# Half of z through another PSUM bank, copied raw, and one product with C fewer on GpSimd in every second group

## What is computed

```python
xz = x @ W_in                                  # x: the layer-normed tokens
xi, z = jnp.split(xz, 2, axis=-1)              # 512 channels each
xc = silu(causal_conv(xi, 4 taps) + conv_b)
dt, Bm, Cm = jnp.split(xc @ W_x, [16, 32], axis=-1)
delta = softplus(dt @ W_dt + b_dt)
h = exp(delta * A) * h + delta * Bm * xc       # for each of 16 states, over the tokens
y = sum_n(h * Cm) + xc * D
out = (y * silu(z)) @ W_out
```

## Time and profile before

| what | us |
|---|---|
| median of 3 runs | 1730.51 |
| lowest, highest | 1729.14, 1731.21 |
| the profiled execution | 1728.77 |
| its span, first to last instruction | 1726.7 |
| busy: PE | 1480.7 (86%) |
| busy: DVE | 1555.7 (90%) |
| busy: ACT | 1331.9 (77%) |
| busy: POOL | 1564.6 (91%) |
| mean granted TensorE clock | 0.947 |

### The profile page before, as it was taken

One profiled execution on the slowest core, in us unless ns is written; L12 is line 12 of the kernel. 1 busy time (PEld: TensorE's weight loads), 2 busy tenths in 40 slices (PEclk: granted clock), 3 DMA queues, 4 the chain that ended last, 5 costly groups with the idle time before them and its releaser, 6 DMA issues.

```text
span 1726.7 us, 28038 instructions
## 1 busy us (share of the span) xinstructions
PE 1480.7 (86%) x9868; PEld 1065.4 (62%) x9868; DVE 1555.7 (90%) x1389; ACT 1331.9 (77%) x3100; POOL 1564.6 (91%) x782
## 2 busy tenths in 40 slices
PE   7778898889888988898889889888889898977688
PEld 7555666666666666666666666666666666654355
DVE  2599999999999999999999999999999999999944
ACT  2577788888888888888888888888888888886644
POOL 0699999999999999999999999999999999999814
PEclk9888999999999999999999999999999999997899
DMA  4667755555656655656666555566665555656110
GB/s 141 138 135 180 163 130 123 122 131 132 145 129 146 132 123 122 131 130 146 129 146 135 122 125 126 130 146 129 145 138 121 125 126 129 142 119 141 36 34 15
DMA packets 194430, 218.47 MB, mean 127 GB/s; under 512 B 94011, under 2 KB 184773, under 8 KB 193778
## 3 DMA queue, kind: packets, MB, share of 16 engines
q1 hardware_dynamic: 193522, 215.51, 56.6%
q0 software_dynamic: 576, 1.17, 0.3%
q10 hardware_dynamic: 192, 0.01, 0.0%
HBM read 169.92 MB, written 47.09 MB: 126 GB/s over the span
## 4 chain that ended last, share of the span: by engine, by line
DVE 41%; ACT 18%; issue 16%; PE 13%; POOL 10%; DMA 2%; SPq 0%; DVEq 0%; ACTq 0%; POOLq 0%
DVE psum L1307 20%; DVE xr L1307 16%; ACT psum L1010 6%; POOL xr L1646 6%; POOL xr L1654 3%; PE psum L610 3%; DVE xr L1316 3%; ACT L1132 2%; PE psum L697 2%; PE psum L782 2%; ACT L1041 2%; ACT soft L1062 2%; ACT soft L1066 2%; ACT soft L1058 2%; PE psum L783 1%
## 5 line engine op out<-in xcount | busy, mean ns | idle before, releaser
L1646 POOL TENSOR_TENSOR xr<-u,bbc 128x912 f32<-128x912 f32 x512 | 1075.5, 2133 | 14.3 <-DMA u<-u_scratch 13.9
L1010 ACT ACTIVATE psum<-delta,a_neg 128x228 f32<-128x228 f32 x2048 | 805.9, 441 | 221.6 <-DVE xr L1316 191.2
L1307 DVE TENSOR_TENSOR_SCAN psum<-psum,xr 128x912 f32<-128x912 f32 x320 | 656.2, 2051 | 68.5 <-ACT psum L1010 59.8
L1654 POOL TENSOR_TENSOR xr<-xr,cbc 128x912 f32<-128x912 f32 x192 | 409.2, 2131 | 31.9 <-DVE xr L1307 28.5
L1307 DVE TENSOR_TENSOR_SCAN xr<-psum,xr 128x912 f32<-128x912 f32 x192 | 392.3, 2043 | 0.0
L1316 DVE TENSOR_TENSOR xr<-psum,cbc 128x912 f32<-128x912 f32 x320 | 353.7, 1105 | 11.1
L711 PE MATMUL psum<-xr,fold 128*32 128x228 f32 x4096 | 295.1, 385 | 50.6 <-POOL xr L1654 26.7
L610 PE MATMUL psum<-xh,win 128*128 128x228 f32 x1024 | 222.7, 367 | 61.8 <-ACT xs L1041 33.4
L610 PEld LDWEIGHTS psum<-xh,win 128*128 128x128 f32 x1024 | 192.1, 193 | 91.7 <-ACT xs L1041 44.0
L661 PE MATMUL psum<-xi,conv_d 128*128 128x228 f32 x1024 | 210.9, 358 | 0.0
L711 PEld LDWEIGHTS psum<-xr,fold 128*32 128x32 f32 x4096 | 96.9, 112 | 178.1 <-issue 79.4
(11 more groups left out here) (204 smaller groups left out, 1574.7 us busy)
## 6 DMA issues: line engine op xcount, KB each, us to landing
delta<-delta_scratch SPq DMA_DIRECT2D x256, 228.0 KB, 6.5
u<-u_scratch SPq DMA_DIRECT2D x256, 228.0 KB, 4.2
bbc<-bc_scratch SPq DMA_DIRECT2D x128, 114.0 KB, 2.6
u_scratch<-u SPq DMA_DIRECT2D x64, 228.0 KB, 4.9
cbc<-bc_scratch SPq DMA_DIRECT2D x128, 114.0 KB, 2.7
delta_scratch<-delta SPq DMA_DIRECT2D x64, 226.0 KB, 5.7
out<-ob SPq DMA_DIRECT2D x32, 228.0 KB
h_scratch<-h SPq DMA_DIRECT2D x31, 228.0 KB
```

What stands on the lines that cost most here:

```text
L1010: ins = nc.scalar.activation(slot(k)[:, j * TOK:(j + 1) * TOK], delta4[:, c // 2, j, c % 2], ACT.Exp, scale=a_neg[:, c, j, n:n + 1])
L1307: nc.vector.tensor_tensor_scan(x if k in ON_POOL else slot(k), slot(k), x, 0.0, ALU.mult, ALU.add).then_inc(scan_done, 1)
L1646: nc.gpsimd.tensor_tensor(xr[:, k % XRING], u4[:, c // 2, :, c % 2], bbc[:, p, n].unsqueeze(1).to_broadcast([P, J, TOK]), ALU.mult).then_i ...
L1654: nc.gpsimd.tensor_tensor(xr[:, k % XRING], xr[:, k % XRING], cbc[:, p, k % NI].unsqueeze(1).to_broadcast([P, J, TOK]), ALU.mult).then_inc ...
```

## The change

Two things are changed. **Half 1 of z** of group g goes into bank BB in place of CB, and is projected right behind unit 7 of the group before, once the transposed rows of the FFN (`x2t`) are copied out of BB. ScalarE copies it as it is into `sz` (`z_copy`, new) behind exponentials 12, and in the window silus it in place, from `sz` to `sz`. `proj_x` half 1, which uses BB next, moves from behind unit 7 to behind unit 8 and waits for that copy. `h2_copy` moves one unit earlier, to 11. There are two counters for z in place of one; waits on `sz_done` are counted anew, and CB is free for tokens after `x_silu` half 0.

**The products with C on GpSimd** are units 1, 3, 8, 10, 12, 13 in even groups (13 in place of 14) and 3, 8, 10, 12, 14 in odd ones (1 is left to VectorE).

```diff
-ON_POOL = (1, 3, 8, 10, 12, 14)
+ON_POOL = (1, 3, 8, 10, 12, 13)
+ON_POOL_ODD = (3, 8, 10, 12, 14)
...
             def z_bank(half):
-                return pair((AB, CB)[half])
+                return pair((AB, BB)[half])
...
                     def bank_c(g):
 
-                        need(pe, xs_done, 2 * g)
-                        need(pe, sz_done, 2 * (g - 1))
+                        need(pe, xs_done, 2 * g - 1)
...
                     def proj_x(g, p, half):
                         if half == 0:
                             pe.wait_ge(xh_done, g + 1)
-                        elif runs(g - 4):
-
-                            pe.wait_ge(x2t_ev, g - 3)
-                        else:
-                            need(pe, delta_done, 2 * g)
+                        elif g >= 1:
+
+                            pe.wait_ge(zc_ev, g)
...
                     def proj_z(g, p, half):
 
-                        if half == 1 and runs(g + 1):
-                            pe.wait_ge(xs_done, 2 * g + 3)
+                        if half == 1 and runs(g - 3):
+                            pe.wait_ge(x2t_ev, g - 2)
                         elif half == 1:
-                            pe.wait_ge(sz_done, 2 * g)
-
+                            pe.wait_ge(delta_done, 2 * g + 2)
...
-                            if k == 13 and runs(i + 1):
-                                proj_z(i + 1, 1 - p, 1)
...
-                            if k == 7 and runs(i + 2):
+                            if k == 7 and runs(i + 1):
+                                proj_z(i + 1, 1 - p, 1)
+                            if k == 8 and runs(i + 2):
                                 proj_x(i + 2, p, 1)
...
-                    def z_silu(g, p, half):
-                        act.wait_ge(z_mm, 2 * g + 1 + half)
-                        need(act, y_done, CH // 2 * (g - 2) + half + 1)
-                        nc.scalar.activation(sz[:, p, 2 * half:2 * half + 2], z_bank(half), ACT.Silu).then_inc(sz_done, 1)
+                    def z_copy(g, p):
+                        act.wait_ge(z_mm[1], g + 1)
+                        need(act, y_done, CH // 2 * (g - 1))
+                        nc.scalar.activation(sz[:, p, 2:], z_bank(1), ACT.Copy).then_inc(zc_ev, 1)
+
+                    def z_silu(g, p):
+                        act.wait_ge(z_mm[0], g + 1)
+                        need(act, y_done, CH // 2 * (g - 2) + 1)
+                        nc.scalar.activation(sz[:, p, 0:2], z_bank(0), ACT.Silu).then_inc(sz_done, 1)
+                        act.wait_ge(zc_ev, g + 1)
+                        nc.scalar.activation(sz[:, p, 2:], sz[:, p, 2:], ACT.Silu).then_inc(sz_b_done, 1)
...
-                            if k == 12 and runs(i - 1):
+                            if k == 11 and runs(i - 1):
                                 h2_copy(i - 1)
...
+                            if k == 12 and runs(i + 1):
+                                z_copy(i + 1, 1 - p)
```

More of the change, by code:

```diff
@@ L49, in fusion_kernel, with on_pool, on_dve, pool_before @@
     E = gate_w.shape[2] - 1
-    ON_DVE = tuple(k for k in range(UNITS) if k not in ON_POOL)
-    N_DVE, N_POOL = len(ON_DVE), len(ON_POOL)
+    def on_pool(i):
+        return (ON_POOL, ON_POOL_ODD)[i % 2]
+    def on_dve(i):
+        return tuple(k for k in range(UNITS) if k not in on_pool(i))
+    def pool_before(i):
+        return sum(len(on_pool(g)) for g in range(i))
+    def dve_before(i):
+        return UNITS * i - pool_before(i)
     bc_scratch = nc.dram_tensor("bc_scratch", (2, 2 * NS, TOK), F32, kind="Internal").ap()
@@ L237, in ffn_free @@
                 elif g == GROUPS - 1:
-                    e.wait_ge(z_mm, 2 * GROUPS)
+                    for half in range(2):
+                        e.wait_ge(z_mm[half], GROUPS)
             def ffn_bank(g):
@@ L344, in fusion_kernel @@
             xs_done = sem("xs_done")
-            z_mm = sem("z_mm")
+            z_mm = [sem("z_mm%d" % half) for half in range(2)]
+            zc_ev = sem("zc_ev")
             sz_done = sem("sz_done")
+            sz_b_done = sem("sz_b_done")
             dbl_mm = sem("dbl_mm")
@@ L436, in product_done @@
             def product_done(e, i, k):
-                if k in ON_POOL:
-                    e.wait_ge(c_pool, N_POOL * i + ON_POOL.index(k) + 1)
+                if k in on_pool(i):
+                    e.wait_ge(c_pool, pool_before(i) + on_pool(i).index(k) + 1)
                 else:
-                    e.wait_ge(c_dve, N_DVE * i + ON_DVE.index(k) + 1)
+                    e.wait_ge(c_dve, dve_before(i) + on_dve(i).index(k) + 1)
             with nc.Block() as block:
@@ L677, in proj_z @@
                             pe.wait_ge(delta_done, 2 * g + 1)
-                        project(p, z_bank(half), (CH + 2 * half) * P).then_inc(z_mm, 1)
+                        project(p, z_bank(half), (CH + 2 * half) * P).then_inc(z_mm[half], 1)
                     def proj_bcdt(g, p):
@@ L693, in proj_delta @@
                         else:
-                            need(pe, sz_done, 2 * g - 1)
+                            need(pe, sz_done, g)
                         for half in range(2):
@@ L739, in h2_turn @@
                         else:
+                            pe.wait_ge(zc_ev, GROUPS)
                             pe.wait_ge(x2t_ev, g)
@@ L752, in ffn_in @@
                             pe.wait_ge(scan_done, UNITS * GROUPS)
-                            pe.wait_ge(c_dve, N_DVE * GROUPS)
+                            pe.wait_ge(c_dve, dve_before(GROUPS))
                         for a in range(2):
@@ L763, in v_center @@
                         if runs(g + 3):
-                            pe.wait_ge(sz_done, 2 * g + 7)
+                            pe.wait_ge(sz_done, g + 4)
                         elif g == GROUPS - 3:
@@ L789, in bias_rows @@
                         pe.wait_ge(pool_c, 4)
-                        pe.wait_ge(sz_done, 2 * GROUPS)
+                        pe.wait_ge(xs_done, 2 * GROUPS)
                         for x in range(E):
@@ L801, in before_first @@
                         var(1)
+                        proj_z(0, 0, 1)
                         for half in range(2):
@@ L805, in before_first @@
                             convolve(1, half)
-                        for half in range(2):
-                            proj_z(0, 0, half)
+                        proj_z(0, 0, 0)
                     def after_last():
@@ L1004, in exps @@
                         step = i if k >= SLOTS else i - 1
-                        if back in ON_POOL:
+                        if step < 0 or back in on_pool(step):
                             need(act, scan_done, v - SLOTS + 1)
                         else:
-                            need(act, c_dve, N_DVE * step + ON_DVE.index(back) + 1)
+                            need(act, c_dve, dve_before(step) + on_dve(step).index(back) + 1)
                         for j in range(J):
@@ L1015, in center_out @@
                         act.wait_ge(cent_mm, g + 1)
-                        need(act, z_mm, 2 * g - 2)
+                        for half in range(2):
+                            need(act, z_mm[half], g - 1)
                         nc.scalar.activation(xh[:, p], pair(CB), ACT.Copy).then_inc(cent_done, 1)
@@ L1129, in window @@
                         if runs(i):
-                            z_silu(i, p, 0)
-                            z_silu(i, p, 1)
+                            z_silu(i, p)
                         act.preload_act_table_set("natural_log_exp_and_others")
@@ L1144, in before_first @@
                         rstd_out(1)
+                        z_copy(0, 0)
                         x_out(1, 0)
@@ L1306, in scan @@
                         x = xr[:, k % XRING].rearrange("p j t -> p (j t)")
-                        nc.vector.tensor_tensor_scan(x if k in ON_POOL else slot(k), slot(k), x, 0.0,
+                        nc.vector.tensor_tensor_scan(x if k in on_pool(i) else slot(k), slot(k), x, 0.0,
                                                      ALU.mult, ALU.add).then_inc(scan_done, 1)
                     def times_c(i, p, k):
-                        if k in ON_POOL:
+                        if k in on_pool(i):
                             return
-                        if k == ON_DVE[0]:
+                        if k == on_dve(i)[0]:
                             dve.wait_ge(c_in, 16 * NQ * (i + 1))
@@ L1650, in times_c @@
                     def times_c(i, p, k):
-                        if k == ON_POOL[0]:
+                        if k == on_pool(i)[0]:
                             pool.wait_ge(c_in, 16 * NQ * (i + 1))
@@ L1684, in body @@
                         for k in range(UNITS):
-                            if runs(i) and k in ON_POOL:
+                            if runs(i) and k in on_pool(i):
                                 times_c(i, p, k)
```

## The result

The change is **slower**: 1776.64 us median (1767.15 to 1783.22, 4 runs) against 1729.83 us before (1729.1 to 1731.21, 4 runs), a ratio of 1.0265 with a 95% interval of 1.0217 to 1.0313. The sign is the one forecast, the size is not: +47 us where +21 was said, and the time lies above the range. The profiled execution took 1777.87 us, with a span of 1776.1 us.

The account below looks back on a forecast made before the run. Bound: VectorE's queue plus its 1.78 us wait for ScalarE before scan 2. Clock +1.2, window -0.42: +0.78 us in 29 groups, -1.5 us for two others, together +21 us: 1751 us, range 1713 to 1764.

Parts of the forecast that it names:

- The sign: Whole kernel: slower, 1751 us against a median of 1730.51; slower by over 0.2% had a chance of 0.62.
- The window and the products: ScalarE's silu window loses its 0.77 us wait for z; the extra VectorE product fits the idle time, cost 0.
- Of the 0.77 us only 0.42 are kept: Scan 4 on VectorE: the centred v does not move with y, so 0.42 us a group are gained.
- TensorE's wait: Before skip_w, with nothing left that does not need y: 2.8 us or more at a stretch, was 0.88.
- The fall of the clock behind it: TensorE's clock falls to 0.50 about when y comes out, over skip_w, fold and centring; path slowed in most groups: 0.57.
- if a low stretch of 3.4 us covers only its start or its end: TensorE's 1.8 us path from y to centred v: about 0.9 us longer then, 1.75 at half speed throughout.
- come up to 1.7 us later ... so I add nothing there: TensorE's tokens, B and C, centring of x: exponentials 6 have 1.6 us in hand, so no cost.
- the path to the centred v at 1.2 us: TensorE's skip_w, fold and centring behind y: 1.2 us longer a group, bounds 0 and 1.75.
- The count: The 29 groups with a centred v (3 to 31) each lose 0.78 us, +22.6 us together.
- Rival 1: The clock holds where y is awaited: 13.7 us gained, 1717 us; chance 0.21.
- Groups 1 and 2: The two early groups without a centred v keep the whole 0.77 us each, -1.5 us together.
- Rival 4: Middle of the group slips, exponentials 13 or 14 late: 0.5 us a group; 1745 us, 1765 with the clock; chance 0.06.

Follow-up runs that it names:

- runs 1 and 6: The kernel before with only the new product sets: 1726.94 us; the change with five unread matmuls in TensorE's wait for y and the old six products: 1709.91 us.
- run 5: The change with five unread matmuls in TensorE's wait for y, and ScalarE's square of the centred v moved behind exponentials 3: 1698.39 us.
- run 3: The change with five unread 228-column matmuls put into TensorE's wait for y, nothing left out: 1709.63 us.
- run 8: The change with the five unread matmuls behind the centring of v, ahead of the tokens, so after the wait for y: 1783.33 us.
- run 9: The change with two unread 228-column matmuls in TensorE's wait for y: 1756.0 us.

## Why the prediction was right and wrong

**The window and the products: right.** Measured from the start of the second y product, the exponentials of state 2 end 0.84 us earlier, and the wait of 1.78 us is 0.93 us. The in-place silu takes 0.61 us, not 0.55. In the window ScalarE no longer waits for half 1 of z; it waits for that projection at the raw copy instead (18.6 us in 26 waits). VectorE does not feel it there: in the short group it idles only ahead of scans 2 and 4. The products cost nothing (runs 1 and 6).

**"Of the 0.77 us only 0.42 are kept": right.** Measured 0.48 us a group where the clock holds (49.26 to 48.78), and 0.38 us more when the square is moved (run 5).

**TensorE's wait: right in one kind of group only.** I reckoned 2.8 us or more. It is 2.60 to 3.36 us ahead of 13 of the 15 long groups and 1.97 to 2.35 us ahead of the 13 short ones. **The fall of the clock behind it: right in kind**, and shown by run 3.

**The size: wrong, in two steps.** The first is "if a low stretch of 3.4 us covers only its start or its end": I took one stretch of 3.4 us, the length that the earlier trace rows shows, for what it would be here too. Behind y it lasts 10.2 us in eleven groups and 13.7 in four. In the earlier trace rows broad matmuls followed (projections, `out_proj`); here the tokens and B and C follow, which use 72 columns of data or 48 of the 128 outputs at a time. Run 8 shows that five broad matmuls ahead of them bring the clock back sooner; which property of the light ones keeps it down, no run separates.

The second step, and the larger, is "come up to 1.7 us later ... so I add nothing there". In the long groups with a centred v the copy of B and C starts 4.4 to 5.7 us later against y. It stands in ScalarE's queue ahead of exponentials 5, and it had nothing in hand, as the trace of before shows: B and C end at 714.40, and their copy starts at 714.44.

```profile
712.66 1.74 PE L685 MATMUL psum<-xs,wx 128*48 128x228 f32 x8
```

```profile
714.44 0.35 ACT L1052 ACTIVATE dbl<-psum 48x228 f32<-48x228 f32 x1
```

The rstd of v behind them was out at 717.10, 0.85 us before VectorE took it (717.95), which is all that the chain had. I had looked at exponentials 6 alone and at their 1.6 us in hand. What I did price, the path to the centred v at 1.2 us, is the smaller part: the square comes 0.1 to 0.5 us later in nine long groups and 1.3 us in the five in which the low stretch begins with y's end.

**The count was wrong the other way**: I put +0.78 us on all 29 groups; 13 groups gained 0.48 us and 15 lost 2.8 to 5.4. The second y products of groups 0 and 31 stand 50.9 us further apart than before (1576.3 against 1525.4 us), although the last two groups gained 5.3 us together.

**Rival 1**, the clock held everywhere, is what run 3 makes of the change: 13.7 us were reckoned and 19.7 measured. Between the same two y products the profile of run 3 is 16.9 us shorter than that of before: 13.3 us in the steady groups and 4.0 in the last two (93.1 against 97.1 us), where I had set the end to 0. Groups 1 and 2, to which I had given 0.77 us each, take 0.4 us more. **Rival 4** has a slip in its sum: 0.5 us a group on top of rival 1 is 1731 us, not 1745.

**What stays open**: which groups are hit. In the change the two kinds of wait named above nearly sort the groups, but two long ones follow a wait of 2.16 us (before 976.00, for one), shorter than the 2.31 us of the short group shown. And with two fillers (run 9) the clock fell behind waits of 1.65 to 2.39 us, while in the change it held behind 1.97 to 2.35. So the length of the wait alone does not decide; what else does, no run shows. The four runs of the change spread over 16 us where those of before spread over 2.

## What to carry to other kernels

An engine with slack is not free to stand still: where TensorE's idle time is gathered in one wait, and the wait ends on the critical path, look at the granted clock of the stretch behind it and at how broad the first matmuls behind it are. Then ask of each result that comes late there how long before its use it is ready today: B and C had 0.04 us, and the rstd behind them 0.85 us. Work that does not depend on the awaited value goes ahead of the wait (here the tokens, which the change itself had set free): 1777 us became 1714, and 1701 with one more step moved. When one wait is removed, look for the next instruction of the same queue that waits for a third engine: here it took 0.35 us of a gain of 0.85, and moving it a place down gave 0.38 back.

## What the runs showed of the hardware

Behind y, the clock came back 3.4 us after it had fallen in 16 of 19 groups where five 228-column matmuls on the full array stood ahead of the tokens (run 8; 6.8 us in the other three). In the change, where tokens (72 columns) and B and C (48 of 128 outputs) followed, it came back only after 10.2 to 13.7 us in 15 groups (6.8 in groups 0 and 29), though TensorE was busy 10.30 of 10.30 us in that stretch. Five unused matmuls, 2.2 us a group, made the kernel 67 us faster; two made it 21 us faster.
